# Cross-attention and FFN block on one core: loads moved into SyncE's timetable, and a new order for every engine

## What is computed

```python
def attn(x, y, mask):                      # x: layernorm of the input, y: (2, 77, 256)
    q = (x @ Wq + bq).reshape(B, 1024, 16, 16)
    k = (y @ Wk + bk).reshape(B, 77, 16, 16)
    v = (y @ Wv + bv).reshape(B, 77, 16, 16)
    att = 0.25 * einsum('bthd,bThd->bhtT', q, k)
    att = softmax(att * mask - 1e10 * (1 - mask))
    return einsum('bhtT,bThd->bthd', att, v).reshape(B, 1024, 256) @ Wo + bo
x = x + attn(layernorm(x), ctx, mask)
t = layernorm(x)
y = t + relu(t @ w1[0] + b1[0]) @ w2[0] + b2[0]
x = x + layernorm(y) * gamma + beta
```

## Time and profile before

| | |
|---|---|
| median of 3 runs | 210.33 us (210.02 to 210.62) |
| span of the profiled execution, first to last instruction | 206.9 us |
| own time of the profiled execution | not recorded apart from the three runs; the median lies 3.4 us above the span |
| PE busy | 188.0 us (91%) |
| VectorE busy | 139.5 us (67%) |
| ScalarE busy | 119.0 us (57%) |
| GpSimd busy | 86.8 us (42%) |
| moved by DMA | 24.72 MB |
| granted TensorE clock, mean | 0.993 |

### The profile page before, as it was taken

One profiled execution on the slowest core, in us unless ns is written; L12 is line 12 of the kernel. 1 busy time (PEld: TensorE's weight loads), 2 busy tenths in 40 slices (PEclk: granted clock), 3 DMA queues, 4 the chain that ended last, 5 costly groups with the idle time before them and its releaser, 6 DMA issues.

```text
span 206.9 us, 3405 instructions
## 1 busy us (share of the span) xinstructions
PE 188.0 (91%) x1202; PEld 148.7 (72%) x1202; DVE 139.5 (67%) x343; ACT 119.0 (57%) x211; POOL 86.8 (42%) x99
## 2 busy tenths in 40 slices
PE   0589887999999979999999999999999999999990
PEld 0374665556667566788899866798888899988990
DVE  2979888688878985359350747177574886277874
ACT  1497545978785888774442699643347720299000
POOL 2467800196615600279739352300484421821121
PEclk9999999999999999999999999999999999999997
DMA  6999598995849265320003002410000020000112
GB/s 203 334 375 361 155 320 236 274 311 202 272 126 338 68 170 167 126 81 0 0 0 82 0 2 78 131 50 0 3 0 0 5 101 0 0 3 0 70 57 76
DMA packets 16336, 24.72 MB, mean 119 GB/s; under 512 B 1728, under 2 KB 7488, under 8 KB 16320
## 3 DMA queue, kind: packets, MB, share of 16 engines
q1 hardware_dynamic: 15056, 23.20, 35.4%
q10 hardware_dynamic: 1264, 1.32, 2.0%
HBM read 14.99 MB, written 8.87 MB: 115 GB/s over the span
## 4 chain that ended last, share of the span: by engine, by line
PE 69%; DMA 17%; DVE 8%; issue 2%; SPq 2%; ACT 0%; POOLq 0%; POOL 0%; DVEq 0%
PE W L777 7%; PE W L763 7%; PE W L780 7%; PE W L778 7%; PE W L765 7%; PE W L764 7%; PE T L700 6%; PE acc L713 5%; DMA Sq<-PT 5%; DMA Sq<-qD 5%; DMA xin<-in_x_dram 5%; PE M L682 3%; PE W L722 3%; DVE xn L959 2%; PE W L745 2%
## 5 line engine op out<-in xcount | busy, mean ns | idle before, releaser
L865 ACT ACTIVATE PT<-T 77x512 f32<-77x512 f32 x64 | 36.2, 592 | 18.1 <-PE T L700 16.6
L777 PE MATMUL W<-w2h,hh 128*128 128x256 f32 x128 | 36.8, 287 | 0.0
L780 PE MATMUL W<-w2h,hl 128*128 128x256 f32 x128 | 36.2, 283 | 0.0
L778 PE MATMUL W<-w2l,hh 128*128 128x256 f32 x128 | 36.2, 283 | 0.0
L1001 DVE TENSOR_REDUCE mx<-M 128x6 fp32r<-128x462 f32 (+1 forms) x48 | 26.3, 580 | 7.2 <-PE M L682 6.8
L907 ACT ACTIVATE hr<-W,cst 128x512 f32<-128x512 f32 x32 | 22.0, 688 | 15.2 <-PE W L765 14.9
L700 PE MATMUL T<-Sq,KS 128*77 128x512 f32 x64 | 25.5, 425 | 3.3 <-DMA Sq<-PT 2.2
L1192 POOL TENSOR_TENSOR hl<-hr,hh 128x512 fp32r<-128x512 f32 x12 | 15.8, 1318 | 30.1 <-ACT hh L911 30.1
L1068 DVE TENSOR_TENSOR hl<-hr,hh 128x512 fp32r<-128x512 f32 x20 | 14.9, 747 | 18.5 <-ACT hh L911 18.4
L777 PEld LDWEIGHTS W<-w2h,hh 128*128 128x128 f32 x128 | 24.5, 191 | 1.8 <-DVE xin L1030 0.8
L763 PE MATMUL W<-x2h,w1h 128*128 128x512 f32 x64 | 25.5, 399 | 0.0
(11 more groups left out here) (112 smaller groups left out, 380.6 us busy)
## 6 DMA issues: line engine op xcount, KB each, us to landing
Sq<-qD SPq DMA_DIRECT2D x16, 384.0 KB, 4.1
qD<-qh SPq DMA_DIRECT2D x8, 512.0 KB, 4.6
qD<-ql SPq DMA_DIRECT2D x8, 256.0 KB, 3.8
xin<-in_x_dram SPq DMA_DIRECT2D x3, 512.0 KB, 9.4
out_dram<-xn SPq DMA_DIRECT2D x6, 256.0 KB, 2.1
Mq<-qD SPq DMA_DIRECT2D x6, 192.0 KB, 2.9
w1raw<-in_L_ffn_w_dram SPq DMA_DIRECT2D x2, 512.0 KB, 12.4
w2raw<-in_L_ffn_w_dram SPq DMA_DIRECT2D x2, 512.0 KB, 14.0
```

Of the source, the lines that this page charges most:

```text
L777: e.matmul(y, hh[:, f, q:q + 128], w2h[:, f * E:(f + 1) * E], start=(f == 0), stop=False)
L778: e.matmul(y, hh[:, f, q:q + 128], w2l[:, f * E:(f + 1) * E], start=False, stop=False)
L780: i = e.matmul(y, hl[:, f, q:q + 128], w2h[:, f * E:(f + 1) * E], start=False, stop=(f == 7))
L865: e.activation(PT[0:TK, m % 6, :], T[m % 2][0:TK, :], ACT.Exp).then_inc(exped, 1)
```

## The change

Three things. First, SP's fixed list of first loads shrinks: wq is issued ahead of x chunk 1, and x chunks 2 and 3 (`xload`), the halves of w1 and w2 (`wload`), become steps with a place in SP's order; so does bo (`late`, 0), which ScalarE's queue issued before. Second, all numbers of TIMES are new, so every engine walks its steps in another order. Third, the assignment of PSUM banks takes and returns the two banks of a `turn` one after the other. No instruction is added or dropped but for the order; lines behind the table move down by 16 to 20 (L1152 is L1171 in the new file).

```diff
 TIMES = {
     "PE": {
-        "idle": "8.4 18.4 22.3",
+        "idle": "4.34 6.06 27.17",
...
     "SP": {
-        "late": "50.1 68.5 69.9 74.8",
+        "late": "45.85 46.44 69.81 71.40 71.99",
+        "xload": "2.71 3.20",
+        "wload": "3.70 4.46 27.64 54.43",
...
             if kind in ("turn", "turn2", "proj"):
                 engine, signal = emptied[kind]
-                for k in range(2):
-                    occupy(step + (k,))
...
                 for k in range(2):
+                    occupy(step + (k,))
                     give_back(step + (k,), engine, step, signal, 2 * (n - 1) + k + 1)
...
+            e.dma_start(wq[:, :, :], wview(wq_bq)).then_inc(ld_wq, 16)
             e.dma_start(xin[:, 4:8, :], x_v[:, row0(1)]).then_inc(ld_x[1], 16)
-            e.dma_start(wq[:, :, :], wview(wq_bq)).then_inc(ld_wq, 16)
-            e.dma_start(xin[:, 8:12, :], x_v[:, row0(2)]).then_inc(ld_x[2], 16)
-            e.dma_start(xin[:, 12:16, :], x_v[:, row0(3)]).then_inc(ld_x[3], 16)
-            for i in range(2):
-                e.dma_start(w1raw[:, F * i:F * i + F], wview(w1[0])[:, i, :]).then_inc(ld_w[i], 16)
-            for i in range(2):
-                e.dma_start(w2raw[:, F * i:F * i + F].rearrange("p (k n) -> p k n", k=4),
-                            wview(w2[0])[:, 4 * i:4 * i + 4, :]).then_inc(ld_w[2 + i], 16)
             for step in walk("SP"):
                 kind, a = step[0], step[1:]
-                if kind == "late":
+                if kind == "xload":
+                    c, = a
+                    e.dma_start(xin[:, 4 * c:4 * c + 4, :], x_v[:, row0(c)]).then_inc(ld_x[c], 16)
+                elif kind == "wload":
+                    i, = a
+                    if i < 2:
+                        e.dma_start(w1raw[:, F * i:F * i + F], wview(w1[0])[:, i, :]).then_inc(ld_w[i], 16)
+                    else:
+                        e.dma_start(w2raw[:, F * (i - 2):F * (i - 1)].rearrange("p (k n) -> p k n", k=4),
+                                    wview(w2[0])[:, 4 * i - 8:4 * i - 4, :]).then_inc(ld_w[i], 16)
+                elif kind == "late":
                     i, = a
                     if i == 0:
+                        e.dma_start(bo_r[:, :], bo.partition_broadcast(P)).then_inc(ld_bo, 16)
+                    elif i == 1:
                         e.dma_start(wo[:, :, :], wview(Wo)).then_inc(ld_wo, 16)
...
             e.dma_start(wv[:, :, :], wview(Wv)).then_inc(ld_wv, 16)
-            e.dma_start(bo_r[:, :], bo.partition_broadcast(P)).then_inc(ld_bo, 16)
```

More of the change, by code:

```diff
@@ L156, in members @@
         return [[(kind, i) for i in range({"kout": 3, "kload": 8}[kind])]]
-    if kind in ("late", "mslot", "sslot", "maskm", "masks"):
-        return [[(kind, i) for i in range({"late": 4, "mslot": 6, "sslot": 8, "maskm": 6, "masks": 8}[kind])]]
+    if kind == "xload":
+        return [[(kind, c) for c in (2, 3)]]
+    if kind in ("wload", "late", "mslot", "sslot", "maskm", "masks"):
+        return [[(kind, i) for i in range({"wload": 4, "late": 5, "mslot": 6, "sslot": 8, "maskm": 6, "masks": 8}[kind])]]
     if kind == "split":
@@ L220 @@
 KINDS = ("idle", "consts", "neg", "flags", "crow", "wqd", "wqh", "wql", "bk4", "kproj", "mask", "mT", "values", "mslot", "sslot",
-         "base", "kout", "kload", "split", "splitwo", "late", "maskm", "masks", "norm", "scale", "turn", "xbias", "qproj", "qlow",
+         "base", "kout", "kload", "xload", "wload", "split", "splitwo", "late", "maskm", "masks", "norm", "scale", "turn", "xbias", "qproj", "qlow",
          "qload", "smax", "mxt", "quadq", "quadm", "st", "pv", "weigh", "attn", "proj", "scale2", "turn2", "bias2", "ffn1",
@@ L496, in sync_program @@
                         mask[0, 0].rearrange("(m p n) t -> p m n t", m=2, n=4)).then_inc(ld_m, 16)
+            e.dma_start(wq[:, :, :], wview(wq_bq)).then_inc(ld_wq, 16)
             e.dma_start(xin[:, 4:8, :], x_v[:, row0(1)]).then_inc(ld_x[1], 16)
-            e.dma_start(wq[:, :, :], wview(wq_bq)).then_inc(ld_wq, 16)
-            e.dma_start(xin[:, 8:12, :], x_v[:, row0(2)]).then_inc(ld_x[2], 16)
-            e.dma_start(xin[:, 12:16, :], x_v[:, row0(3)]).then_inc(ld_x[3], 16)
-            for i in range(2):
-                e.dma_start(w1raw[:, F * i:F * i + F], wview(w1[0])[:, i, :]).then_inc(ld_w[i], 16)
-            for i in range(2):
-                e.dma_start(w2raw[:, F * i:F * i + F].rearrange("p (k n) -> p k n", k=4),
-                            wview(w2[0])[:, 4 * i:4 * i + 4, :]).then_inc(ld_w[2 + i], 16)
             for step in walk("SP"):
                 kind, a = step[0], step[1:]
-                if kind == "late":
+                if kind == "xload":
+                    c, = a
[8 more added lines that the diff above has]
+                elif kind == "late":
                     i, = a
                     if i == 0:
+                        e.dma_start(bo_r[:, :], bo.partition_broadcast(P)).then_inc(ld_bo, 16)
+                    elif i == 1:
                         e.dma_start(wo[:, :, :], wview(Wo)).then_inc(ld_wo, 16)
-                    elif i == 1:
+                    elif i == 2:
                         e.dma_start(b2_r[:, :], b2[0].partition_broadcast(P)).then_inc(ld_b2, 16)
-                    elif i == 2:
+                    elif i == 3:
                         e.dma_start(be_r[:, :], beta.partition_broadcast(P)).then_inc(ld_be, 16)
```

## The result

The changed kernel takes 227.37 us (median of 4 runs, 224.77 to 229.81), the kernel before 210.48 on the same chip. The ratio is 1.073 (95% interval 1.065 to 1.080); it leaves disturbed runs out and is therefore smaller than that of the medians. The forecast was 209.2 us, in a range of 207.2 to 211.8.

What follows compares the result with a forecast made beforehand. TensorE's work plus 25.9 us of waiting was taken as the bound up to the last FFN2 step. Head +1.2, attention -2.0, rest -0.3 made -1.1 us, so 209.2 us from a median of 210.33; range 207.2 to 211.8.

Steps and rivals of the forecast that it cites:

- The head, wq pair and copies: Head, GpSimd: wq pair at 12.84 us after wqb, then five mask copies, root of chunk 1 done at 18.3, before 15.4.
- "16.7 us" of VectorE: Head: VectorE's work from 18.3 us to the maximum that frees the first mxt, at 35.0; scalings taken at 1.37 each.
- The way from there to T<-Sq: End of head: mxt, copy and issue 0.5 us, the maxima's way to Sq 2.5; first T<-Sq at 38.0.
- four DMA round trips that no order shortens: Attention stretch: the sixteen T<-Sq of chunk 0 take 14.5 us, as before.
- The next links: Attention stretch: 4.7 us to the second attn transpose (before 8.9), then 1.5 to proj (before 4.6).
- "8.0" from proj to turn2: Attention stretch, chunk 0: proj to turn2 takes 8.0 us, before 10.6.
- From turn2 to FFN1: End of attention stretch: turn2 to the first FFN1 takes 3.7 us, before 4.5.
- The rest, 0.3 better ... everything behind it is in order: First FFN1 to last FFN2 step: waiting 3.3 us, before 3.6; bounds 2.1 and 4.5.
- The offset: Whole kernel: the median lies 3.4 us above the profiled span, and this difference is kept.
- (c): Head: pauses leave TensorE at 1.2 GHz, chunk 0's qproj pairs take near 3.6 us; 211.4 us with 2.2 us; chance 0.27.
- (b): Head doesn't slip: wqb lands sooner, wq pair starts before 11.5 us, head 0.4 us better; 207.6 us, chance 0.15.
- (d): Middle: freed filler is worth nothing, waits move to chunks 2 and 3, head and middle cancel; 210.3 us, chance 0.13.

Runs made afterwards that it cites:

- e1: The changed kernel with only VectorE's centring of the first half of chunk 2 put back behind three low parts of chunk 3: 220.78 us, ratio 1.051.
- e4: The changed kernel with seven more idle steps on TensorE, placed in its pauses in the head: 224.84 us, ratio 1.070.
- e3: The changed kernel with GpSimd's five mask copies ahead of the wq difference again: 224.53 us, ratio 1.066.
- x8: e6 with SyncE's second Sq load of chunk 0 moved ahead of the first load of maxima: 216.49 us, ratio 1.033.
- e6: The changed kernel with four repairs: centring back, mask copies ahead, seven idle steps added, w2 halves among the first loads: 217.51 us, ratio 1.035.
- e2: The changed kernel with both w2 halves among SyncE's first loads again, right behind w1: 225.22 us, ratio 1.074.
- x7: e6 with GpSimd's bias addition for chunk 1 moved ahead of the root of chunk 0: 216.43 us, ratio 1.032.
- x9: e6 without the seven idle steps: 220.18 us, ratio 1.041.
- y1: e6 with both the bias addition of x7 and the Sq load of x8 moved: 213.72 us, ratio 1.0175.
- x10: The kernel before in its old order, with wq ahead of x chunk 1 and bo moved to SyncE's queue, w2 among the first loads: 210.51 us, ratio 1.004.
- h1: Hybrid: changed kernel's order up to the first T<-Sq, the order of the kernel before behind it, all weights among the first loads: 219.99 us, ratio 1.048.

## Why the prediction was wrong, step by step

**The head, wq pair and copies: right.** The pair waited for wqb (13.84, forecast 12.84), the five copies and the root followed, x_rs was done at 19.3 (forecast 18.3). The 1.0 us between them is wqb itself, landing at 13.7 instead of 12.7; in e1 and e4, where the pair started at 12.97, x_rs was done at 18.4. What the copies' place costs in all, e3 doesn't show clear of noise (0.7%).

**The head, "16.7 us" of VectorE: mis-sized.** From x_rs to the last maximum ahead of mxt were 19.8 us. (The terms listed add up to 16.5 and not 16.7.) The scalings, taken at 1.37 each from the earlier trace rows, took 1.92 and 2.62 beside GpSimd, and the trace of the kernel before had one of 2.63 at 18.10; one kl took 1.13 and not 0.3; and VectorE waited 0.5 us for TensorE's maxima. The way from there to T<-Sq took 2.6 us and not 3.0. First T<-Sq 41.8, forecast 38.0.

**The attention chain, "four DMA round trips that no order shortens": this step failed.** It is true, and I used it as if no order could lengthen them. They took 18.9 us, not 14.5. SyncE's second Sq load stood behind steps that wait for the maxima (x8: 1.7 us); a lower clock from 49.9 to 53.3 made 512-column matmuls of 0.23 us ones of 0.43 (about 1.5 us by e6 and e3, which have no fall there). The other 1.2 us are not assigned. The next links were right: 4.7 (4.7) to the second attn transpose, 1.5 (1.5) to proj.

**"8.0" from proj to turn2: failed too.** It was 12.0. Two things made it longer. The second w2 half, which I said had cover since FFN2 comes late, is split by ScalarE ahead of chunk 1's exponentials: I named the last reader and not the engine that had to read it in order. And the scaling took 3.94 us and not 1.4, because the new order put GpSimd's 2.6 us of bias beside it. The half out of the way gave 1.4 us (e2, e6), the bias 1.9 more; with both out of the way the link took 8.7 (x7), near the forecast. From turn2 to FFN1 were 4.1 (forecast 3.7).

**"The rest, 0.3 better ... everything behind it is in order": failed.** I had taken the wall of matmuls from the earlier trace rows as a property of the kernel. It is one of the order: VectorE's centring ahead of the split cost 4.6 us (e1), the lower clock behind the wait included. The measured 9.6 us of waiting, against 3.3, have another 1.4 us that nothing here explains.

**The offset.** The 3.4 us that I kept between span and median were not a constant of the program: the time of an execution lies about 1.8 us above its own span. This moves the forecast by nothing, since the change was added to the median of before.

**The rivals.** (c), the clock, had the right mechanism for a small part: one qproj pair took 3.75 us (I had said both), the clock fell four times and not once, and the idle steps against it are worth about 0.6% with the rest mended (x9, e6), within the intervals. (b) is refuted, the pair didn't start early. (d) is nearer to what happened in the middle, but had no loss behind 80 us. None of the four had a loss of more than 2.2 us: each link was priced as if the links beside it stayed at the lengths of the old order.

**A mechanism beneath three of the failed terms** (the scalings of the head, the scaling of chunk 0, the centring) is VectorE beside GpSimd. The instructions of one form show it, here the four scalings of chunk 0 in the changed kernel (shortest, median and longest in ns):

```profile
L1075 DVE TENSOR_SCALAR xn<-xin,mv,rs x4: 695/1054/1364, 75.0 to 78.2; 128x256 f32<-128x256 f32 x4
```

In the kernel before the four took 1.37 us together; x7 took GpSimd's bias away and got 2.02 us for the four. The Trainium skill (SBUF — State Buffer, SBUF: two separate sides) says that GpSimd shares one pair of SBUF ports with VectorE, and that one of the two holds it exclusively for a whole instruction when VectorE is in a two-port mode, or has two SBUF inputs while GpSimd reads SBUF. The trace agrees: a scaling beside GpSimd grew from 0.41 to 1.36 us and a centring from 0.48 to 1.5, about the length of one of GpSimd's instructions (1.29 to 1.45 us); a TENSOR_SCALAR of 128x2, started at 189.99, took 1.04 us and ended with GpSimd's addition; and those that read PSUM did not grow (the two at 193.86 took 1.28 us beside the same additions). Which mode VectorE's scaling ran in, no run here shows.

**What stays open:** how much of the 5.4 us by which the first T<-Sq of y1 is still late could be won back, where copies, idle steps and loads were already mended. VectorE's 5.1 us more of work ahead of the first mxt stand against it, and with them the clock. The steps that the new order puts there include VectorE's norm, scaling and split of chunk 3. Moving the last two behind the maxima of chunk 0 was not tried, so this last part is read from the trace and not shown by a run.

## What to carry to other kernels

When a whole order is exchanged, don't price the forecast chain alone: walk each in-order queue for the steps that now stand *ahead* of a link (SyncE's loads, VectorE's and ScalarE's steps that nobody waits for soon) and ask what each waits for. Lay GpSimd's SBUF instructions beside VectorE's critical SBUF ones: here each such meeting lengthened an instruction of VectorE by about 1 us. And a single repair of a worse order may show nothing: mend the links of one chain together (x7 and x8 with y1) before calling one harmless. Before you compare one stretch of two profiles, look whether the clock fell in it, since one fall was worth as much here as a repair.

## What had not been expected of the hardware

- wqb, the same transfer behind the same ones of its own queue, landed anywhere from 12.70 to 14.28 us in the profiles of these kernels.
- The load of 8 KB of maxima behind the second w2 half took 6.9 us in the changed kernel (e1 6.9, e3 6.8, e4 5.5), and 3.8 to 4.7 us in the runs of that order whose w2 halves were first; the median of all 16 such loads is 1.8 us. Loads and stores of other tiles ahead can do the same: 6.6 us in x10 and 6.9 in h1 without a w2 half.
- A granted clock of 1.00 in a stretch doesn't show that TensorE ran at 2.4 GHz. The traces have no record of the clock ahead of a first one (at 20.0 us in x9, 13.0 in the kernel before, 9.0 in the changed kernel, 12.9 in e1), and a stretch without a record reads 1.00. The matmuls ahead of that record have the lengths of 1.2 GHz: in x9 the first qproj pair, at 15.82, took 3.75 us and the second, at 20.19, 1.88; in the earlier trace rows two idle matmuls took 2.02 us at 8.39 and 1.02 at 18.77. So in x9 the clock had not fallen, it had not yet risen.
